# Weighing the values head by head, with four key blocks in the four column groups of TensorE

## The chip, the cores and the metric

The kernel runs on one core of a Trainium2 chip. The metric is the device time of one launch in microseconds. Three runs of the kernel before gave 10604.21, 10606.17 and 10610.16 us; their median is 10606.17.

## The reference, cut to what matters

One layer stack over x of shape [16, 512, 128]: attention with 16 heads of 8 channels, a mixture of 8 experts, a state-space block solved by 8 fixed-point turns, and the mixture once more, each behind a layer norm and added to x. The change touches the attention alone:

```python
scores = jnp.einsum('bhqd,bhkd->bhqk', q, k) * SCALE
weights = jax.nn.softmax(scores, axis=-1)
attn = jnp.einsum('bhqk,bhkd->bhqd', weights, v)
attn = attn.transpose(0, 2, 1, 3).reshape(B, T, D)
return attn @ out_w + out_b
```

## The kernel before, in words

The five engines each run their own program and meet at semaphores; nothing reorders them, so the order written in the loops is the order on each queue. A loop runs over the 16 batch elements. In each come the attention, the mixture, the state-space block (the longest part, with 8 turns), and the mixture again; the preparation of the next element's queries, keys and values (`start`, ten steps on VectorE) is laid into the last mixture.

The attention of one element has 512 tokens in four blocks of 128. A loop over h (steps 0 to 19) runs on TensorE, ScalarE and VectorE at once. In step h:

- TensorE scores head h (`score`, L492, four products into the banks 0 to 2 in turn), VectorE takes the row maxima (`rowmax`, L1292), and splits them into two bf16 parts (`split_max`).
- The maximum of head h-1 is turned (`turn_max`, L502) into two rows of bank 6 and copied beside the queries (`copy_max`), by ScalarE in the steps with even h (L937) and by VectorE in those with odd h (L1306), between the third and the fourth exp or row maximum.
- Head h-2 is scored again, keys down and queries across, with the maximum subtracted (`rescore`, L515, banks 3 and 4 in turn), and ScalarE takes the exp into `probsT` (`exp`, L945). A re-scoring waits for the exp two before it, since there are two banks.
- Queries and keys of head h+2 are turned into bank 5 (`turn_head`, L479) and ScalarE copies them to `heads` (`copy_head`, L932).

Weighing (`weigh`, L527) goes by four heads (HG = 4). When the probabilities of heads 4c to 4c+3 are there, the step has four visits, one for each block of 128 keys. A visit is four products of 512 columns, one for each head, with 32 columns of `vaug` as the stationary operand (8 value channels, a column of ones that gives the sum of the weights, and zeros). Head j of the four writes partitions 32j to 32j+31 of bank 7, so the four run side by side in the four column groups, and the four visits add up in the bank. Then ScalarE copies the bank to `oT` (`copy_out`, L950), TensorE turns its four blocks back into bank 7 (`turn_out`, L535), and VectorE divides by the sums (`normalise`, L1313 and L1316). After the last group the result is turned (L557), copied (L966) and projected (L561), and VectorE adds it to x (L1333).

The values are laid into `vaug` in step 9 of `start` (L1282 and L1284): the area was filled with zeros earlier, then the column of ones, then one copy of all heads.

Of the kernel before, what the change touches and what calls it, by code (L numbers as in the profile page):

```python
# [14 lines left out]
P = 128  # L15
# [8 lines left out]
TB = T // P  # L24
NH, HD = 16, 8
HG = 4
# [85 lines left out]
def hybrid_kernel(nc, t, out):  # L112

    with ExitStack() as ctx:
# [90 lines left out]
        probsT = piece(HG * TB * T).rearrange("p (j k t) -> p j k t", j=HG, k=TB)  # L205
# [58 lines left out]
        vchain = signal("vchain", 44, 8, 20)  # L264
# [12 lines left out]
        nchain = signal("nchain", 7)  # L277
# [20 lines left out]
        o_copied = signal("o_copied", NH // HG)  # L298
        o_turned = signal("o_turned", NH // HG)
        o_normed = signal("o_normed", NH // HG)  # L300
# [144 lines left out]
        def _(eng):  # L445
# [22 lines left out]
            def attention(at):  # L468
# [27 lines left out]
                def turn_max(h):  # L496

                    eng.wait_ge(max_parts.sem, max_parts.count(at, h + 1))
                    if h > 0:
                        eng.wait_ge(max_copied.sem, max_copied.count(at, h))  # L500
                    for tb in range(TB):
                        mm = eng.matmul(ps[BIAS:BIAS + 2, 6, tb * P:(tb + 1) * P],  # L502
                                        smax_b[:, h % 2, tb, :], ident_b[:],
                                        start=(tb == 0), stop=(tb == TB - 1))
                    mm.then_inc(max_turned.sem, max_turned.up(at))
# [391 lines left out]
        def _(eng):  # L897
# [26 lines left out]
            def attention(at):  # L924
# [10 lines left out]
                def copy_max(h):  # L935
                    eng.wait_ge(max_turned.sem, max_turned.count(at, h + 1))
                    eng.activation(heads[BIAS:BIAS + 2, h % QUAD, 0], ps[BIAS:BIAS + 2, 6, :],  # L937
                                   ACT.Copy).then_inc(max_copied.sem, max_copied.up(at))

                def exp(h, kb):  # L940
                    eng.wait_ge(rescored.sem, rescored.count(at, TB * h + kb + 1))
                    if h >= HG and h % HG == 0:

                        eng.wait_ge(weighed.sem, weighed.count(at, h - HG + kb + 1))
                    eng.activation(probsT[:, h % HG, kb, :], bank(3 + (TB * h + kb) % 2), ACT.Exp,  # L945
                                   scale=SCALE).then_inc(exped.sem, exped.up(at))

                def copy_out(c):
                    eng.wait_ge(weighed.sem, weighed.count(at, TB * (c + 1)))
# [4 lines left out]
                for h in range(NH + AHEAD + 2):  # L954
# [220 lines left out]
        def _(eng):  # L1175
# [31 lines left out]
            def start(at, step):  # L1207
# [71 lines left out]
                if step == 9:  # L1279

                    eng.wait_ge(v_zero.sem, v_zero.count(at, 1))
                    eng.memset(vaug[:, :, :, HD:HD + 1], 1.0).then_inc(nchain.sem, nchain.up(at))  # L1282
                    eng.wait_ge(nchain.sem, nchain.last(at))
                    eng.tensor_copy(  # L1284
                        vaug[:, :, :, 0:HD], qkv[:, :, 2 * DM:].rearrange("p b (h c) -> p b h c", c=HD)
                            ).then_inc(v_ready.sem, v_ready.up(at))

            def attention(at):
# [15 lines left out]
                def copy_max(h):  # L1304
                    eng.wait_ge(max_turned.sem, max_turned.count(at, h + 1))
                    eng.tensor_copy(heads[BIAS:BIAS + 2, h % QUAD, 0], ps[BIAS:BIAS + 2, 6, :]  # L1306
                                    ).then_inc(max_copied.sem, max_copied.up(at))

                def normalise(c):

                    eng.wait_ge(o_turned.sem, o_turned.count(at, c + 1))
                    o = blocks(7).rearrange("p b (j r) -> p b j r", r=32)
                    eng.reciprocal(rsum[:], o[:, :, :, HD]).then_inc(vchain.sem, vchain.up(at))  # L1313
                    eng.wait_ge(vchain.sem, vchain.last(at))
                    dst = attn[:, :, c * HG * HD:(c + 1) * HG * HD].rearrange("p b (j r) -> p b j r", r=HD)
                    eng.tensor_tensor(  # L1316
                        dst, o[:, :, :, 0:HD],
                        rsum[:].rearrange("p b (j o) -> p b j o", o=1).broadcast_to([P, TB, HG, HD]),
                        ALU.mult).then_inc(o_normed.sem, o_normed.up(at))

                for h in range(NH + AHEAD + 2):
# [8 lines left out]
                    if behind > HG and behind % HG == 1:  # L1330
                        normalise(behind // HG - 1)
                eng.wait_ge(projected.sem, projected.count(at, 1))
# [411 lines left out]
```

## Time and profile before

| | |
|---|---|
| median of three runs | 10606.17 us |
| the profiled execution itself | 10630.49 us |
| its span | 10628.6 us |
| mean granted TensorE clock | 0.958 |
| TensorE busy | 9367.1 us (88%) |
| VectorE busy | 9021.3 us (85%) |
| ScalarE busy | 7321.0 us (69%) |
| GpSimd busy | 6111.1 us (57%) |

The profile is of one execution. An engine's share is its busy time over the span; a product on TensorE is pipelined, so its record (0.39 us for a product of 512 bf16 columns) overlaps the next one's, and the pace is read from the starts. PEclk is the share of the full TensorE clock (2.4 GHz) that was granted; 0.50 is 1.2 GHz. An f32 product has two records, an f32 turned block one. The first element's attention lies between 43 and 125 us of the span and each later one about 661 us after the one before.

### The profile page before, as it was taken

The page shows a single profiled execution, that of the slowest core. Times are in us where ns is not written, and L with a number is a line of the kernel's source. Part 1 is how long each engine was busy: PE and PEld are TensorE (multiplying, and loading weights), DVE is VectorE, ACT ScalarE, POOL GpSimd, SP SyncE. Part 2 cuts the span into 40 slices and gives each one's busy share as a digit, 9 for nine tenths or more (in the row PEclk, how much of TensorE's full clock was granted, in tenths as well). Part 3 has the DMA queues.
Part 4 walks back from the last instruction along what each step waited for, and adds up shares of the span by engine and source line. Part 5 has one row for each costly group of instructions (what it writes and reads, how often), then busy time and mean ns, then how long its engine had stood idle before and what let it go on. Part 6 is the DMA issues. An engine that isn't in the chain of part 4 may idle for free.

```text
span 10628.6 us, 254158 instructions
## 1 busy us (share of the span) xinstructions
PE 9367.1 (88%) x86042; PEld 6259.7 (59%) x86042; DVE 9021.3 (85%) x16781; ACT 7321.0 (69%) x15068; POOL 6111.1 (57%) x4900
## 2 busy tenths in 40 slices
PE   7988889888898888988889888898888988889888
PEld 4656656566565665656656566565665656656566
DVE  6978979788797887978879798797987979879798
ACT  5867768677685776857767576675766857668576
POOL 1936728367293672926729277292762927639276
PEclk9999999999999999999999999999999999999999
DMA  0000000000000000000000000000000000000000
GB/s 21 0 3 1 1 3 0 3 1 1 3 0 3 1 2 3 0 3 1 2 3 0 3 1 1 3 0 3 1 1 3 0 3 1 2 3 0 3 1 3
DMA packets 648462, 23.40 MB, mean 2 GB/s; under 512 B 629185, under 2 KB 647250, under 8 KB 647506
## 3 DMA queue, kind: packets, MB, share of 16 engines
q1 hardware_dynamic: 647890, 16.11, 3.6%
q8 instruction: 318, 5.21, 0.2%
q14 instruction: 254, 2.08, 0.1%
HBM read 9.40 MB, written 4.19 MB: 1 GB/s over the span
## 4 chain that ended last, share of the span: by engine, by line
DVE 31%; PE 27%; issue 17%; POOL 15%; ACT 5%; DVEq 2%; DMA 1%; POOLq 1%; SPq 0%; ACTq 0%
DVE work L1563 15%; POOL work L1662 15%; DVE work L1553 6%; PE ps L579 4%; PE ps L584 4%; PE ps L594 3%; PE ps L527 2%; PE ps L515 2%; PE ps L788 1%; ACT da L945 1%; DMA hend<-work 1%; PE ps L492 1%; PE ps L654 1%; DVE stats L1185 1%; DVEq L1547 1%
## 5 line engine op out<-in xcount | busy, mean ns | idle before, releaser
L1662 POOL TENSOR_TENSOR work<-work,crep 128x512 f32<-128x512 f32 x4608 | 5767.5, 1275 | 4437.9 <-DVE work L1502 3820.5
L1061 ACT ACTIVATE scan_in<-du,bcn 128x256 f32<-128x256 f32 x8832 | 3685.7, 497 | 18.1 <-PE ps L788 13.6
L1563 DVE TENSOR_TENSOR_SCAN work<-da,hend,ps 128x256 f32<-128x256 f32 x4608 | 3037.4, 724 | 45.1 <-PE ps L788 22.3
L788 PE MATMUL ps<-w_ident,scan_in 128*128 128x128 f32 x18432 | 2722.0, 282 | 325.4 <-ACT scan_in L1061 111.3
L788 PEld LDWEIGHTS ps<-w_ident,scan_in 128*128 128x128 f32 x18432 | 2034.1, 143 | 1286.9 <-issue 724.3
L1553 DVE TENSOR_TENSOR_SCAN work<-da,ps 128x512 f32<-128x512 f32 x2048 | 2364.1, 1200 | 19.1 <-PE ps L788 2.4
L778 PE MATMUL ps<-work,w_sel 128*32 128x256 f32 x17792 | 1410.2, 393 | 157.0 <-POOL work L1662 146.2
L979 ACT ACTIVATE work<-ps,w_gate_b 128x512 f32<-128x512 f32 x512 | 351.8, 687 | 895.2 <-PE ps L579 894.7
L1292 DVE TENSOR_REDUCE smax<-ps 128x1 f32<-128x512 f32 x1024 | 661.1, 686 | 201.5 <-PE ps L492 197.5
L778 PEld LDWEIGHTS ps<-work,w_sel 128*32 128x32 f32 x17792 | 355.5, 108 | 619.3 <-POOL work L1662 370.3
L945 ACT ACTIVATE da<-ps 128x512 f32<-128x512 f32 x1024 | 572.9, 596 | 164.1 <-PE ps L515 157.4
L1393 DVE SCALAR_TENSOR_TENSOR work<-ps,w_up_b,work 128x512 f32<-128x512 f32 x512 | 377.8, 750 | 271.8 <-PE ps L584 225.4
L742 PE MATMUL ps<-w_ident,bcn 128*32 128x128 f32 x18432 | 579.8, 279 | 0.0
L579 PE MATMUL ps<-xnT,gate_w 128*128 128x512 f32 x1024 | 567.1, 637 | 0.0
L584 PE MATMUL ps<-xnT,up_w 128*128 128x512 f32 x1024 | 552.3, 622 | 0.0
L594 PEld LDWEIGHTS ps<-down_w,work 128*128 128x128 f32 x4096 | 489.8, 192 | 88.3 <-issue 68.9
L742 PEld LDWEIGHTS ps<-w_ident,bcn 128*32 128x32 f32 x18432 | 507.3, 112 | 47.0 <-issue 44.3
L1077 ACT ACTIVATE yscT<-ps 128x512 f32<-128x512 f32 x288 | 172.0, 597 | 502.9 <-PE ps L778 502.9
L594 PE MATMUL ps<-down_w,work 128*128 128x128 f32 x4096 | 501.0, 276 | 4.0 <-DVE work L1393 4.0
L1045 ACT ACTIVATE u_sb<-ps 128x512 f32<-128x512 f32 x256 | 153.0, 598 | 498.6 <-DVE du L1518 498.6
L723 PE MATMUL ps<-mix_y,yT 128*128 128x256 f32 x2048 | 485.5, 380 | 0.0
L515 PE MATMUL ps<-da 98*128 98x512 bf16 x1024 | 394.6, 389 | 102.5 <-ACT da L945 59.5
(201 smaller groups left out, 12259.1 us busy)
## 6 DMA issues: line engine op xcount, KB each, us to landing
hend<-work SPq DMA_DIRECT2D x2304, 1.0 KB, 1.8
x_in<-in_x SPq DMA_DIRECT2D x17, 256.0 KB, 2.8
out<-work SPq DMA_DIRECT2D x16, 256.0 KB
gate_w<-in_gate_w SPq DMA_DIRECT2D x1, 1024.0 KB, 5.4
up_w<-in_up_w SPq DMA_DIRECT2D x1, 1024.0 KB, 7.5
down_w<-in_down_w SPq DMA_DIRECT2D x1, 1024.0 KB, 9.4
w_w_zy<-in_w_zy SPq DMA_DIRECT2D x1, 256.0 KB
work<-in_w_mix SPq DMA_DIRECT2D x1, 256.0 KB
```

What stands on the lines that cost most here:

```text
L579: mm = eng.matmul(bank(u % 2), gate_w[:, e, f * P:(f + 1) * P], xnT[:], start=True, stop=True)
L584: mm = eng.matmul(bank(2 + u % 2), up_w[:, e, f * P:(f + 1) * P], xnT[:], start=True, stop=True)
L594: mm = eng.matmul(blocks(6 + e % 2)[:, tb, :], hid[:, e % 2, f, tb * P:(tb + 1) * P], down_w[:, e, f, :], start=(tb == 0 and f == 0), stop ...
L742: mm = eng.matmul(ps[GC * k:GC * (k + 1), bank + m // 2, c:c + P], bcn[:, hf, tb, 1, n:n + 1].broadcast_to([P, GC]), ident[:], start=(m % ...
L778: mm = eng.matmul(ps[GC * q:GC * (q + 1), 3, j % 2 * TH:(j % 2 + 1) * TH], w["sel"][:], prod[:, p % PROD, q % 2 * TH:(q % 2 + 1) * TH], st ...
L788: mm = eng.transpose(ps[:, bank, c:c + P], scan_in[:, m, tb, 2 * j + s].rearrange("p k c -> p (k c)"), ident[:])
L945: eng.activation(probsT[:, h % HG, kb, :], bank(3 + (TB * h + kb) % 2), ACT.Exp, scale=SCALE).then_inc(exped.sem, exped.up(at))
L1061: ins = eng.activation(scan_in[:, m, tb, :, k, :], du[:, hf, tb, :].rearrange("p (e c) -> p e c", c=GC), ACT.Copy, scale=bcn[:, hf, tb, 0, ...
L1292: eng.tensor_reduce(smax[:, h % 2, qb:qb + 1], bank(u % 3), AX, ALU.max).then_inc(maxed.sem, maxed.up(at))
L1553: eng.tensor_tensor_scan(hst[:, p % NHID, :], da[:, 0, 2 * p:2 * p + 2, :].rearrange("p s t -> p (s t)"), bank(RING[p % 4]), 0.0, ALU.mult ...
L1563: ins = eng.tensor_tensor_scan(hst[:, p % NHID, half], da[:, 1, 2 * p + s, :], ps[:, RING[p % 4], half], hend[:, 2 * p + s:2 * p + s + 1], ...
L1662: eng.tensor_tensor(prod[:, to, :].rearrange("p (s t) -> p s t", s=2), hst[:, p % NHID, :].rearrange("p (s t) -> p s t", s=2), crep[:, hf, ...
```

## The change

Weighing goes head by head. For head h the four products of a visit are its four blocks of keys, each in a column group of its own, so that the four groups hold partial sums. Three heads share bank 7 (HG = 3): head h has its 9 columns (8 channels and the sum) at 9 times (h mod 3) of the 32, zeros elsewhere, and the three add up in the bank. Sixteen heads make six groups (OUTS = 6), the last with one head. The probabilities stay in a ring of four heads (HR = 4). The turning multiplies by `sel`, four unit matrices of 32 stacked, which turns a block of tokens and adds the four partial sums at once, into 128 columns of bank 6; the turned maximum moves from bank 6 to bank 5. The copy of the values into `vaug` becomes three fills and three copies, one pair for each place.

In TensorE's loop `weigh(h-3)` stands after the second re-scoring of step h, from step 3 on; `weigh(15)` and the last two turnings stand behind the loop. Core of the diff:

```diff
-HG = 4
+HG = 3
+HR = 4
+OUTS = -(-NH // HG)
+HC = HD + 1
@@ TensorE
-                def weigh(c, kb):
-                    eng.wait_ge(exped.sem, exped.count(at, TB * (HG * c + HG - 1) + kb + 1))
-                    if c == 0 and kb == 0:
+                def weigh(h):
+                    eng.wait_ge(exped.sem, exped.count(at, TB * (h + 1)))
+                    if h == 0:
                         eng.wait_ge(v_ready.sem, v_ready.count(at, 1))
-                    if c > 0 and kb == 0:
-                        eng.wait_ge(o_normed.sem, o_normed.count(at, c))
-                    for j in range(HG):
-                        mm = eng.matmul(ps[32 * j:32 * j + 32, 7, :],
-                                        vaug[:, kb, HG * c + j, :], probsT[:, j, kb, :],
-                                        start=(kb == 0), stop=(kb == TB - 1))
+                    if h > 0 and h % HG == 0:
+                        eng.wait_ge(o_copied.sem, o_copied.count(at, h // HG))
+                    for kb in range(TB):
+                        mm = eng.matmul(ps[32 * kb:32 * kb + 32, 7, :],
+                                        vaug[:, kb, h, :], probsT[:, h % HR, kb, :],
+                                        start=(h % HG == 0), stop=(h % HG == HG - 1 or h == NH - 1))
                     mm.then_inc(weighed.sem, weighed.up(at))
 
                 def turn_out(c):
                     eng.wait_ge(o_copied.sem, o_copied.count(at, c + 1))
+                    if c > 0:
+                        eng.wait_ge(o_normed.sem, o_normed.count(at, c))
                     for tb in range(TB):
-                        mm = eng.transpose(blocks(7)[:, tb, :], oT[:, tb * P:(tb + 1) * P], ident[:])
+                        mm = eng.matmul(ps[:, 6, tb * GC:(tb + 1) * GC], oT[:, tb * P:(tb + 1) * P],
+                                        w["sel"][:], start=(tb == 0), stop=(tb == TB - 1))
...
-                for h in range(NH + AHEAD + 2):
+                for h in range(NH + AHEAD):
...
-                        if behind >= HG and behind % HG == 0:
-                            weigh(behind // HG - 1, b)
                         if 0 <= behind < NH:
                             rescore(behind, b)
+                        if b == 1 and behind >= 1:
+                            weigh(behind - 1)
                     if h + 2 < NH:
                         turn_head(h + 2)
-                    if behind > HG and behind % HG == 1:
+                    if behind >= HG + 1 and behind % HG == 1:
                         turn_out(behind // HG - 1)
-                eng.wait_ge(o_normed.sem, o_normed.count(at, NH // HG))
+                weigh(NH - 1)
+                turn_out(OUTS - 2)
+                turn_out(OUTS - 1)
+                eng.wait_ge(o_normed.sem, o_normed.count(at, OUTS))
@@ ScalarE
                 def copy_out(c):
-                    eng.wait_ge(weighed.sem, weighed.count(at, TB * (c + 1)))
+                    eng.wait_ge(weighed.sem, weighed.count(at, min(HG * (c + 1), NH)))
+                    if c > 0:
+                        eng.wait_ge(o_turned.sem, o_turned.count(at, c))
...
+                copy_out(OUTS - 1)
@@ VectorE, start step 9
-                    eng.memset(vaug[:, :, :, HD:HD + 1], 1.0).then_inc(nchain.sem, nchain.up(at))
-                    eng.wait_ge(nchain.sem, nchain.last(at))
-                    eng.tensor_copy(
-                        vaug[:, :, :, 0:HD], qkv[:, :, 2 * DM:].rearrange("p b (h c) -> p b h c", c=HD)
-                            ).then_inc(v_ready.sem, v_ready.up(at))
+                    v = qkv[:, :, 2 * DM:].rearrange("p b (h c) -> p b h c", c=HD)
+                    for j in range(HG):
+                        eng.memset(vaug[:, :, j:NH:HG, HC * j + HD:HC * (j + 1)], 1.0)
+                    for j in range(HG):
+                        ins = eng.tensor_copy(vaug[:, :, j:NH:HG, HC * j:HC * j + HD], v[:, :, j:NH:HG, :])
+                    ins.then_inc(v_ready.sem, v_ready.up(at))
```

`normalise(c)` on VectorE keeps its place behind the maxima of the step in which `turn_out(c)` stands, reads 27 columns a block (9 for the last group) from bank 6, and the last one stands behind the loop.

## Rows read from the trace of the kernel before

**Rows 1.** The page's chain that ended last: shares by engine, then by line.
```profile
DVE 31%; PE 27%; issue 17%; POOL 15%; ACT 5%; DVEq 2%; DMA 1%; POOLq 1%; SPq 0%; ACTq 0%
DVE work L1563 15%; POOL work L1662 15%; DVE work L1553 6%; PE ps L579 4%; PE ps L584 4%; PE ps L594 3%; PE ps L527 2%; PE ps L515 2%; PE ps L788 1%; ACT da L945 1%; DMA hend<-work 1%; PE ps L492 1%; PE ps L654 1%; DVE stats L1185 1%; DVEq L1547 1%
```
**Rows 2.** Windows of the first attention: length, busy of PE, PEld, DVE, ACT, POOL, clock.
```profile
60.00:67.00 7.00, 6.26 (x47) 3.02 (x44) 6.77 (x15) 6.95 (x12) 0.00 (x0) 1.00 0.00 1
67.00:74.00 7.00, 7.00 (x55) 1.93 (x55) 3.89 (x10) 4.12 (x8) 0.00 (x0) 1.00 0.00 0
111.00:115.00 4.00, 2.09 (x9) 0.67 (x9) 0.73 (x4) 3.59 (x8) 0.00 (x0) 1.00 0.00 0
115.50:118.50 3.00, 3.00 (x17) 0.80 (x20) 0.00 (x0) 0.60 (x1) 0.00 (x0) 0.50 0.00 0
```
**Rows 3.** Timeline of ScalarE, two quiet steps of the last element: start, length, line.
```profile
9979.83 2.16 ACT L945 ACTIVATE da<-ps 128x512 f32<-128x512 f32 x4
...
9982.78 1.67 ACT L945 ACTIVATE da<-ps 128x512 f32<-128x512 f32 x3
9984.47 0.59 ACT L937 ACTIVATE da<-ps 2x512 bf16<-2x512 f32 x1
...
9986.48 2.16 ACT L945 ACTIVATE da<-ps 128x512 f32<-128x512 f32 x4
```
**Rows 4.** Timeline, the end of the first attention, and one row of the last.
```profile
115.70 0.60 ACT L945 ACTIVATE da<-ps 128x512 f32<-128x512 f32 x1 [0.21 <-PE ps L515]
...
120.72 0.60 ACT L950 ACTIVATE work<-ps 128x512 f32<-128x512 f32 x1 [4.43 <-PE ps L527]
...
122.71 0.66 PE L557 MATMUL ps<-w_ident,work 128*128 128x128 f32 x4 [0.68 <-DVE work L1316]
...
10040.57 0.60 ACT L950 ACTIVATE work<-ps 128x512 f32<-128x512 f32 x1 [3.00 <-PE ps L527]
```
**Rows 5.** Groups by line: count, busy us, mean ns, idle before and its releaser.
```profile
L950 ACT ACTIVATE work<-ps 128x512 f32<-128x512 f32 x64 | 38.0, 593 | 68.0 <-PE ps L527 68.0
```
**Rows 6.** Timeline of TensorE in the first burst, and one row of the second.
```profile
68.32 0.38 PE L492 MATMUL ps<-da 96*128 96x512 bf16 x1
...
68.63 1.06 PE L527 MATMUL ps<-da,scan_in 128*32 128x512 f32 x8
...
69.63 0.39 PE L515 MATMUL ps<-da 98*128 98x512 bf16 x1
...
85.64 1.07 PE L527 MATMUL ps<-da,scan_in 128*32 128x512 f32 x8
```
**Rows 7.** Timeline of TensorE in a quiet step of the first element.
```profile
78.62 0.39 PE L502 MATMUL ps<-ident_b,smax_b 128*2 128x128 bf16 x4
78.94 0.39 PE L515 MATMUL ps<-da 98*128 98x512 bf16 x1
79.16 0.38 PE L492 MATMUL ps<-da 96*128 96x512 bf16 x1
...
79.60 0.61 PE L479 MATMUL ps<-ident_b,da 128*72 128x128 bf16 x8
80.05 0.38 PE L492 MATMUL ps<-da 96*128 96x512 bf16 x1
```
**Rows 8.** Timeline, step 2 of the first element: fourth exp, and the re-scoring it frees.
```profile
56.93 0.60 ACT L945 ACTIVATE da<-ps 128x512 f32<-128x512 f32 x1
...
57.59 0.39 PE L515 MATMUL ps<-da 98*128 98x512 bf16 x1
```
**Rows 9.** Timeline of TensorE in the state-space block: f32 products of 32 columns.
```profile
244.25 0.98 PE L714 MATMUL ps<-w_w_bc,yT 128*128 128x32 f32 x8
245.07 0.31 PE L788 MATMUL ps<-w_ident,scan_in 128*128 128x128 f32 x1
```
**Rows 10.** Timeline of VectorE before the second element's first row maxima.
```profile
702.81 0.43 DVE L1284 COPY scan_in<-scan_in 128x512 f32<-128x512 f32 x1
...
706.65 2.48 DVE L1292 TENSOR_REDUCE smax<-ps 128x1 f32<-128x512 f32 x4 [3.40 <-PE ps L492]
```

More of the change, by code:

```diff
@@ L262, in hybrid_kernel @@
         stored = signal("stored", behind=1, unit=16)
-        vchain = signal("vchain", 44, 8, 20)
+        vchain = signal("vchain", 46, 8, 20)
         class Norm:
@@ L297, in hybrid_kernel @@
         weighed = signal("weighed", NH)
-        o_copied = signal("o_copied", NH // HG)
-        o_turned = signal("o_turned", NH // HG)
-        o_normed = signal("o_normed", NH // HG)
+        o_copied = signal("o_copied", OUTS)
+        o_turned = signal("o_turned", OUTS)
+        o_normed = signal("o_normed", OUTS)
         a_turned = signal("a_turned", 1)
@@ L936, in copy_max @@
                     eng.wait_ge(max_turned.sem, max_turned.count(at, h + 1))
-                    eng.activation(heads[BIAS:BIAS + 2, h % QUAD, 0], ps[BIAS:BIAS + 2, 6, :],
+                    eng.activation(heads[BIAS:BIAS + 2, h % QUAD, 0], ps[BIAS:BIAS + 2, 5, :],
                                    ACT.Copy).then_inc(max_copied.sem, max_copied.up(at))
@@ L941, in exp @@
                     eng.wait_ge(rescored.sem, rescored.count(at, TB * h + kb + 1))
-                    if h >= HG and h % HG == 0:
-                        eng.wait_ge(weighed.sem, weighed.count(at, h - HG + kb + 1))
-                    eng.activation(probsT[:, h % HG, kb, :], bank(3 + (TB * h + kb) % 2), ACT.Exp,
+                    if h >= HR and kb == 0:
+                        eng.wait_ge(weighed.sem, weighed.count(at, h - HR + 1))
+                    eng.activation(probsT[:, h % HR, kb, :], bank(3 + (TB * h + kb) % 2), ACT.Exp,
                                    scale=SCALE).then_inc(exped.sem, exped.up(at))
                 def copy_out(c):
-                    eng.wait_ge(weighed.sem, weighed.count(at, TB * (c + 1)))
+                    eng.wait_ge(weighed.sem, weighed.count(at, min(HG * (c + 1), NH)))
+                    if c > 0:
+                        eng.wait_ge(o_turned.sem, o_turned.count(at, c))
                     eng.activation(oT, bank(7), ACT.Copy).then_inc(o_copied.sem, o_copied.up(at))
@@ L953, in attention @@
                 copy_head(1)
-                for h in range(NH + AHEAD + 2):
+                for h in range(NH + AHEAD):
                     behind = h - AHEAD
@@ L1305, in copy_max @@
                     eng.wait_ge(max_turned.sem, max_turned.count(at, h + 1))
-                    eng.tensor_copy(heads[BIAS:BIAS + 2, h % QUAD, 0], ps[BIAS:BIAS + 2, 6, :]
+                    eng.tensor_copy(heads[BIAS:BIAS + 2, h % QUAD, 0], ps[BIAS:BIAS + 2, 5, :]
                                     ).then_inc(max_copied.sem, max_copied.up(at))
@@ L1311, in normalise @@
                     eng.wait_ge(o_turned.sem, o_turned.count(at, c + 1))
-                    o = blocks(7).rearrange("p b (j r) -> p b j r", r=32)
-                    eng.reciprocal(rsum[:], o[:, :, :, HD]).then_inc(vchain.sem, vchain.up(at))
+                    n = min(HG, NH - HG * c)
+                    o = ps[:, 6, 0:TB * GC].rearrange("p (b r) -> p b r", r=GC)[:, :, 0:n * HC].rearrange(
+                        "p b (j r) -> p b j r", r=HC)
+                    eng.reciprocal(rsum[:, :, 0:n], o[:, :, :, HD]).then_inc(vchain.sem, vchain.up(at))
                     eng.wait_ge(vchain.sem, vchain.last(at))
-                    dst = attn[:, :, c * HG * HD:(c + 1) * HG * HD].rearrange("p b (j r) -> p b j r", r=HD)
+                    dst = attn[:, :, c * HG * HD:(c * HG + n) * HD].rearrange("p b (j r) -> p b j r", r=HD)
                     eng.tensor_tensor(
                         dst, o[:, :, :, 0:HD],
-                        rsum[:].rearrange("p b (j o) -> p b j o", o=1).broadcast_to([P, TB, HG, HD]),
+                        rsum[:, :, 0:n].rearrange("p b (j o) -> p b j o", o=1).broadcast_to([P, TB, n, HD]),
                         ALU.mult).then_inc(o_normed.sem, o_normed.up(at))
-                for h in range(NH + AHEAD + 2):
+                for h in range(NH + AHEAD + 1):
                     behind = h - AHEAD
@@ L1329, in attention @@
                         split_max(h)
-                    if behind > HG and behind % HG == 1:
+                    if behind >= HG + 1 and behind % HG == 1:
                         normalise(behind // HG - 1)
+                normalise(OUTS - 1)
                 eng.wait_ge(projected.sem, projected.count(at, 1))
```

6 lines of the change are left out of this document (3 added, 3 removed).

## The prediction

> **What bounds the kernel now.** I read the page's totals and its chain first. TensorE is the busiest (88% of the span), but the chain is shared: VectorE 31%, TensorE 27%, and of the attention lines only L527 (weighing) and L515 (re-scoring) reach 2% each [rows 1]. So the change touches one stage of each of the 16 batch elements, and that stage has to be read by itself. A batch element takes about 661 us; its attention runs from 43 to 125 us in the first.
>
> The stage's windows show two kinds of steps (a step is one turn of the head loop, h; it scores head h and re-scores head h-2). In the quiet ones, without weighing, ScalarE is busy 6.95 of 7 us and VectorE 6.77 [rows 2]: ScalarE sets the pace. A step in which it copies no maximum takes 2.95 us (first exp at 9979.83 to first exp at 9982.78), one with it 3.70 (to 9986.48), 3.33 on average [rows 3]. In the burst, where four heads are weighed in one step, TensorE is busy 7.00 of 7 us while VectorE has 3.89 and ScalarE 4.12 [rows 2]. Four steps with one burst take 17.0 us (a group of weighings at 68.63, the same group of the next four heads at 85.64), 4.25 a step [rows 6]. At the end nothing is left beside the last burst: the last exp begins at 115.70, ScalarE copies the result at 120.72, and the final turning begins at 122.71 [rows 4]. TensorE runs that burst at half clock, 0.50 granted from 115.5 to 118.5, that is 1.2 GHz, after four microseconds in which it was busy 2.09 of 4 [rows 2]. The last element keeps 2.4 GHz there, and its copy waits 3.00 us instead of 4.43 [rows 4]. The copies' idle time is 68.0 us in all [rows 5]; at 3.00 and about 4.45 that makes 14 slow tails and 2 fast ones.
>
> **The change, part by part.** It doesn't lessen the weighing: 64 products of 512 columns before and after. It spreads them, one group of four side by side per step from step 3 on, adds two rounds of copying, turning and normalising (6 for 4), and makes the turning a real product.
>
> *Weighing on TensorE.* In the burst a group starts 0.31 us after the score ahead of it (68.32 to 68.63) and the next product 1.00 us later (69.63), where two plain products stand 0.22 apart [rows 6, 7]. A group therefore costs 0.31 + 1.00 - 0.22 = 1.09 us. Its columns alone are 0.89 of it: its records last 1.06, and a plain product's record of 0.39 outlasts the next start by 0.17; 0.20 is the change from plain products to groups and back. I take 1.09 in the new place too, between a re-scoring and a score. Bounds: 0.89, and 1.3 if the 0.20 came twice.
>
> The Trainium skill, TensorEngine Tiling (Array Packing), Key Properties, says that changing the tiling mode drains TensorE, which speaks against sixteen separate visits. By that rule, and the trace agrees with its 0.20 us a visit, the sixteen weighings keep their 1.09 each; without a drain the sum would be 3.2 us an element less.
>
> *A step of TensorE.* I call R1 the start of a step's second re-scoring and R2 of its third. From R1: 0.31 to the weighing, 1.00 to the score, 0.31 to the turned maximum (as to the weighing), 0.32 to R2 (78.62 to 78.94) [rows 6, 7]: 1.94. From R2 three products of 0.22, the head's turning 0.45 (79.60 to 80.05), three more of 0.22 to the next R1 [rows 7]: 1.77. A step is 3.71 if nothing waits. ScalarE (2.95 or 3.70 [rows 3], and at most the 0.59 of a copied result [rows 5] more) and VectorE (6.77 us in a little over two quiet steps [rows 2], and some 0.2 for each step's share of normalising) are under that, so TensorE becomes the bound. One wait is added on it: re-scoring product 1 needs the previous head's last exp. On even steps ScalarE has the copied maximum between exps 2 and 3: R2, exp 0.43 later (the product's record is 0.39), the maximum 0.61 later and the last exp 0.61 after that (each takes 0.59 to 0.60), then 0.66 to the product it frees (56.93 to 57.59) [rows 3, 8]: 0.43 + 0.61 + 0.61 + 0.66 = 2.31 in place of 1.77. An even step is 1.94 + 2.31, or 4.24, an odd one 3.71.
>
> *The new turning.* Before it is four turned blocks in one load each; now four products with an f32 block of 128 columns loaded twice each. The nearest row is L714, 128x128 f32 against 32 columns: eight records, the next product 0.82 us after their start [rows 9]. It stands at the end of steps 6, 9, 12 and 15. Even steps hide 0.53 of it in ScalarE's wait, so 0.29 + 0.82 + 0.29 = 1.40 for the first three. Bounds: 0.44 each (the four turned blocks of before, at the 0.45 that eight smaller ones of a head take) and 1.0. The copy of the result (0.59) on ScalarE is new for two of the six; the weighing behind it waits for it by 0.17 once in steps 3 to 13.
>
> *Adding up.* R1 of step 3 is at 57.59 [rows 8] and stays there. Five even and six odd steps: 5 x 4.24 + 6 x 3.71 = 43.5, with 1.40 and 0.17: R1 of step 14 at 102.6. Step 14 even: R1 of 15 at 106.9; the weighing there waits for the copy until 107.3; R2 108.95, turning, R1 of 16 at 110.7; weighing and maximum, R2 112.3; exp, maximum, exp: the third exp of ScalarE at 113.95; R1 of 17 at 114.6; weighing, R2 115.9; last exp 116.9 to 117.5. Now a chain that is all new: copy 0.6 (118.0), weigh head 15 1.0 (119.0), turn 1.0 (120.0), and the last round of copy, turning, reciprocal and product, which before takes 1.99 (120.72 to 122.71) and 0.3 more with the longer turning: the final turning at 122.3, against 122.71 [rows 4]. So at full clock the gain is 0.4 us an element, and all of it is the slow clock that before paid (about 1.45 in 14 of 16). Against the two fast elements it loses 1.2.
>
> *The clock.* From 113 to 118 the laid-out TensorE is busy some 2.4 of 5 us, no more than in the stretch before which it fell before [rows 2]. I take it that it falls again, about when head 15 is weighed: 1.0 to 1.6 us, 1.3. Then an element loses 0.9 in 14 cases and 1.2 in 2: 15 us.
>
> *The values' preparation.* One fill and one copy become three and three on VectorE: four instructions more, each under the 0.43 of today's whole copy, so at most 1.7 us. VectorE then idles 3.40 us before its first maximum, waiting for TensorE [rows 10]. Nothing. The maximum's move to bank 5 moves no work; I price it at nothing, since its product and its copy stay where they are; were its copy to wait for a head's copy (1.0 us) it would add at most that in each step, and nothing in the change asks for that.
>
> Sum against the profiled execution, 10628.6 of span and 10630.5 in all: +15, 10645. The runs shown have their median 24 us under it, at 10606.2; the same 15 us give 10621.
>
> **The rivals.** The measurement tells about 0.2%, 21 us, from no change: 1.3 us an element.
> A, the clock stays up: TensorE has work in every step to the end. For it: the last element kept it. Against: 14 didn't, with the same busy share. -0.4 x 14 + 1.2 x 2 = -3: 10603.
> B, the weighing hides better than in the burst: its loads come early beside plain products and it costs its columns alone, 0.89. For it: the loads of a group are short and there are plain products on both sides to hide them. Against: the 0.31 and 1.00 of the groups now, which also stand between plain products [rows 6]. 0.20 x 16 = 3.2 an element, 51 less than the forecast: 10570. Faster.
> C, slower: the slow stretch falls over the new end chain, from the weighing of head 14 to the last turning. Weighings +0.9 twice, turnings +0.8 twice (their columns and loads again): 3.4, less the 0.4: 3.0 x 16 = 48, 10654. It decides from two of these four on. For it: the chain's gaps (copies of 0.6 between short products) leave TensorE less than half busy; against: it came back after 3.3 us before.
> D, the four groups don't run side by side: 2.6 us a head more, 656 in all, 11260. Against: L527 does so in the same groups now.
>
> **How the numbers follow.** Forecast 0.37, A 0.15, B 0.24, C 0.22, D 0.02. Likeliest 10621, which is no change that can be told (+0.14%); with the bounds of the turning (0.4 x 6 an element at most, partly hidden, about 1.5 x 16 = 24 either way) it has its own range of 10600 to 10645. Over B and C the range is 10563 to 10656. Faster: B, and a little of A, 0.26. Slower: C, D and the upper part of the forecast's range, 0.31. The same: 0.43.
>
> **What would show it.** Steps 3 to 13 at 4.24 and 3.71 in turn: the head copies of ScalarE (L932) tell. Near 3.33 or 3.7 throughout: B, the wait for the exp was wrong. TensorE's idle waits for the exp should grow only on even steps. L714's 0.82 should return in the new turning. The final turning of the first element (122.7 now) is the yardstick: at 122.3 with granted clock 1.00 around the last weighing is A, 123.6 with 0.50 is the forecast, beyond 125 is C. Wrong altogether if the stage outside attention moves.

## The result and the profile after

The changed kernel takes 10659.53 us, the median of 5 runs (10658.40 to 10668.38), against 10606.17 before (10599.39 to 10610.16): a ratio of 1.0053, interval 1.0039 to 1.0068. It is slower by 53 us where no change was forecast, and 3.5 us beyond the range. The profiled execution took 10668.38 (span 10666.5, mean granted clock 0.952 for 0.958), 38 us over the profiled one of before.

The page after, busy time by engine and then the chain's shares. They hardly differ from [rows 1]: the page as a whole doesn't tell where 53 us went.

```profile
PE 9434.6 (88%) x86554; PEld 6343.1 (59%) x86554; DVE 9036.0 (85%) x16913; ACT 7330.6 (69%) x15100; POOL 6116.0 (57%) x4900
...
DVE 33%; PE 29%; issue 17%; POOL 13%; ACT 3%; DMA 2%; DVEq 2%; POOLq 1%; SPq 0%; ACTq 0%
```

So I measured each stage in all 16 elements, from VectorE's and ScalarE's instructions at its two ends, and took means (us):

```
stage of an element                              before   after
first head copy to add of the projection          79.29   81.50
  of it: first head copy to final turning         76.7    77.56
first half of the first mixture                   17.94   18.39
end of an element to the next one's first copy     0.82    1.29
scan iterations, all eight                       374.25  373.64
rest of the state-space block (inputs, tail)      65.69   65.63
at half clock: end of attention                    3.05    5.73
at half clock: start of the first mixture          7.19   11.34
```

Attention is 2.21 us an element longer, 35 in all; 0.9 of the 2.21 lies ahead of the final turning, the rest behind it.

The body of attention. Timeline of TensorE in the first element after (start, length, engine, line, operands); L518 re-scores, L540 is the new turning, L495 scores. The first four L518 rows are R1, the start of the second re-scoring, of four steps in turn.

```profile
62.48 0.38 PE L518 MATMUL ps<-da 98*128 98x512 bf16 x1
...
66.12 0.39 PE L518 MATMUL ps<-da 98*128 98x512 bf16 x1 [0.20 <-ACT da L946]
...
66.74 0.39 PE L518 MATMUL ps<-da 98*128 98x512 bf16 x1
...
70.47 0.38 PE L518 MATMUL ps<-da 98*128 98x512 bf16 x1
...
73.52 1.03 PE L540 MATMUL ps<-w_sel,work 128*128 128x32 f32 x8
74.39 0.38 PE L495 MATMUL ps<-da 96*128 96x512 bf16 x1
...
75.05 0.38 PE L518 MATMUL ps<-da 98*128 98x512 bf16 x1
```

From 62.48 to 66.74 is an even step, 4.26 us (the row at 66.12 is not an R1: it is the re-scoring that waited for ScalarE's copied maximum, L946); to 70.47 an odd one, 3.73; to 75.05 an even one with a turning, 4.58. The turning's visit costs 0.87 (73.52 to 74.39). Medians over the 16 elements of steps 3 to 13 are 3.72, 4.26, 3.72, 4.58, 3.71, 4.26, 4.75, 4.26, 3.72, 4.58, 3.71, in sum 45.27.

The end of attention. Timeline of the first element after; this execution reached its first head copy 0.84 us later than the one of before (46.57 against 45.73), so 0.84 is to be taken off before a row is laid beside [rows 4].

```profile
117.71 1.08 ACT L954 ACTIVATE da<-ps 128x512 f32<-128x512 f32 x2 [0.72 <-PE ps L518]
118.68 0.60 ACT L961 ACTIVATE work<-ps 128x512 f32<-128x512 f32 x1
...
119.34 1.06 PE L530 MATMUL ps<-da,scan_in 128*32 128x512 f32 x8 [1.45 <-ACT work L961]
...
120.33 1.08 PE L540 MATMUL ps<-w_sel,work 128*128 128x32 f32 x8
121.45 0.60 ACT L961 ACTIVATE work<-ps 128x512 f32<-128x512 f32 x1 [2.16 <-PE ps L540]
...
122.12 1.88 PE L540 MATMUL ps<-w_sel,work 128*128 128x32 f32 x8 [0.71 <-ACT work L961]
...
124.50 1.12 PE L566 MATMUL ps<-w_ident,work 128*128 128x128 f32 x4 [0.50 <-DVE work L1331]
...
126.30 2.07 PE L570 MATMUL ps<-w_out_w,work 128*128 128x128 f32 x8 [0.69 <-ACT work L978]
...
128.41 0.69 DVE L1349 TENSOR_TENSOR x_res<-ps,x_res 128x512 f32<-128x512 f32 x1 [3.97 <-PE ps L570]
```

The same stretch before, from the projection on:

```profile
124.05 1.16 PE L561 MATMUL ps<-w_out_w,work 128*128 128x128 f32 x8 [0.69 <-ACT work L966]
125.24 0.69 DVE L1333 TENSOR_TENSOR x_res<-ps,x_res 128x512 f32<-128x512 f32 x1 [2.59 <-PE ps L561]
```

Three pieces run at nearly twice the length that they have at full clock: the last turning 1.88 for 1.08, the final turning 1.12 for 0.66 [rows 4], the projection 2.07 for 1.16. Windows of the two kernels (length, busy of PE, PEld, DVE, ACT, POOL, then the granted clock), after first and then before, say why:

```profile
115.00:119.00 4.00, 2.31 (x12) 0.46 (x12) 0.00 (x0) 3.26 (x7) 0.00 (x0) 1.00 0.00 0
119.00:123.00 4.00, 2.96 (x21) 2.03 (x21) 0.49 (x2) 0.88 (x2) 0.00 (x0) 0.89 0.00 0
123.00:127.00 4.00, 2.81 (x12) 2.27 (x13) 0.38 (x2) 1.33 (x2) 0.00 (x0) 0.50 0.00 0
127.00:131.00 4.00, 1.37 (x7) 1.08 (x6) 2.11 (x11) 0.84 (x2) 0.00 (x0) 0.50 0.00 0
```

```profile
119.00:123.00 4.00, 2.59 (x23) 0.96 (x16) 0.55 (x2) 0.60 (x1) 0.00 (x0) 1.00 0.00 0
123.00:127.00 4.00, 1.52 (x12) 1.09 (x10) 1.68 (x8) 1.88 (x2) 0.00 (x0) 1.00 0.00 0
127.00:131.00 4.00, 2.07 (x8) 1.47 (x9) 1.55 (x9) 1.76 (x3) 0.00 (x0) 0.72 0.00 0
```

Before, the slow stretch began under the burst [rows 2] and was over by 119; the final turning, the projection and the first products of the mixture had 2.4 GHz (in 15 of the 16 elements; in the last a slow stretch begins under the projection). After, the burst is gone, the clock falls about 122.1 (0.89 granted from 119 to 123 is 0.9 us at half), and all that chain runs at 1.2 GHz. So it goes in all 16 elements after. Only the last turning is caught to different extents: 1.88 us in the first element, 1.59 in the mean, 1.06 at full clock (a_warm below). The groups by line carry it over all elements (count, then busy us, mean ns of one, and idle before with its releaser); after, then before:

```profile
L518 PE MATMUL ps<-da 98*128 98x512 bf16 x1024 | 385.5, 384 | 54.3 <-ACT da L946 37.4 <-DVE da L1319 10.3 <-ACT da L954 3.7
L530 PE MATMUL ps<-da,scan_in 128*32 128x512 f32 x2048 | 272.7, 605 | 26.2 <-ACT work L961 23.2
...
L570 PE MATMUL ps<-w_out_w,work 128*128 128x128 f32 x128 | 33.2, 441 | 11.0 <-ACT work L978 11.0
...
L566 PE MATMUL ps<-w_ident,work 128*128 128x128 f32 x64 | 17.9, 435 | 8.1 <-DVE work L1331 8.1
...
L1349 DVE TENSOR_TENSOR x_res<-ps,x_res 128x512 f32<-128x512 f32 x16 | 11.1, 691 | 63.5 <-PE ps L570 63.5
```

```profile
L561 PE MATMUL ps<-w_out_w,work 128*128 128x128 f32 x128 | 19.0, 292 | 11.0 <-ACT work L966 11.0
...
L1333 DVE TENSOR_TENSOR x_res<-ps,x_res 128x512 f32<-128x512 f32 x16 | 11.1, 692 | 41.9 <-PE ps L561 41.9
L557 PE MATMUL ps<-w_ident,work 128*128 128x128 f32 x64 | 10.5, 286 | 10.8 <-DVE work L1316 10.8
```

VectorE's wait from the last normalisation to the add (L1349, before L1333) is 63.5 us in all for 41.9, that is 3.97 an element for 2.62. The 21.6 us between them lie in the final turning and the projection, at 435 and 441 ns a product for 286 and 292. L518 waits 37.4 of its 54.3 us behind the copied maximum (L946), and L530 waits 23.2, 1.45 an element, for the copy of the result ahead of head 15 (L961).

### The profile page after: what moved, and what is told of

Its sections match the earlier page's. It is cut to its first block, busy times and chain, and to the rows that moved or that the text cites. A ratio compares the mean times of both kernels' runs of the same rounds, so it can differ in the third digit from the quotient of the medians.

```text
span 10666.5 us, 255586 instructions
## 1 busy us (share of the span) xinstructions
PE 9434.6 (88%) x86554; PEld 6343.1 (59%) x86554; DVE 9036.0 (85%) x16913; ACT 7330.6 (69%) x15100; POOL 6116.0 (57%) x4900
## 3 DMA queue, kind: packets, MB, share of 16 engines
q14 instruction: 270, 2.21, 0.1%
## 4 chain that ended last, share of the span: by engine, by line
DVE 33%; PE 29%; issue 17%; POOL 13%; ACT 3%; DMA 2%; DVEq 2%; POOLq 1%; SPq 0%; ACTq 0%
DVE work L1579 17%; POOL work L1678 12%; DVE work L1569 6%; PE ps L588 4%; PE ps L593 4%; PE ps L603 3%; PE ps L530 2%; PE ps L518 2%; DMA hend<-work 2%; PE ps L495 2%; DVE stats L1197 1%; PE ps L797 1%; PE ps L663 1%; DVEq L1563 1%; PE ps L540 1%
## 5 line engine op out<-in xcount | busy, mean ns | idle before, releaser
L518 PE MATMUL ps<-da 98*128 98x512 bf16 x1024 | 385.5, 384 | 54.3 <-ACT da L946 37.4
```

Source lines behind the costliest of these rows:

```text
L518: mm = eng.matmul(bank(3 + u % 2), k[:, kb * P:(kb + 1) * P], q, start=True, stop=True)
```

## The experiments

Eight kernels ran, in two sets; each set has its own runs of the kernel before (medians 10626.87 of 21 runs, and 10614.0 of 15), and ratios are against these. The expected times were set against 10606.17; the first set's runs of before are 20.7 us higher, so there ratios are to be compared. By them b_warm and a_early lie in theory 1's range, a_warm just under its lower edge (0.9988 for 0.9989 to 1.0015), and a_own below both of its ranges (0.9976, and neither goes under 1.0004). The filler products in three of the eight are bf16 products of 512 columns into PSUM bank 1, which nobody reads at that time; they stand in TensorE's program where it would wait, and change only how busy it is.

**a_warm**: the changed kernel with fillers from the last re-scorings to behind the projection.

```diff
+                def busy(n):
+                    for _ in range(n):
+                        eng.matmul(bank(1), ident_b[0:BIAS, :], heads[0:BIAS, 0, 1], start=True, stop=True)
...
+                        if behind == NH - 1 and b == 0:
+                            busy(3)
...
+                busy(5)
                 weigh(NH - 1)
                 turn_out(OUTS - 2)
+                busy(2)
                 turn_out(OUTS - 1)
+                busy(2)
...
                 mm.then_inc(a_turned.sem, a_turned.up(at))
+                busy(2)
...
                 mm.then_inc(projected.sem, projected.up(at))
+                busy(11)
```

> The changed kernel, with idle stretches of TensorE at the end of each attention filled: 25 bf16 products of 512 columns (0.22 us each) whose result nobody reads, 3 ahead of the re-scoring of head 15, 5 ahead of the weighing of head 15, 2 ahead of the last turning, 2 ahead of the final turning, 2 ahead of the projection, 11 behind it. They add nothing to the computation. Theory 1 (the loss is the slow clock): the clock stays at 1.00 from the last weighing to the projection, the last turning, the final turning and the projection give back 0.9 + 0.46 + 0.91 = 2.3 us an element, attention falls from 81.5 to about 79.2 us and the start of the mixture with it: 10595 to 10622. Theory 2 (the loss is the new end chain and the longer turning by themselves, the slow clock comes along without costing): within 10 us of the changed kernel, 10650 to 10670.

Measured: 10610.61, ratio 0.9988 (0.9979 to 0.9997). Against the changed kernel's 1.0053 the fillers gain 0.65%. The same end, timeline of TensorE and VectorE of this kernel:

```profile
121.06 1.06 PE L540 MATMUL ps<-w_sel,work 128*128 128x32 f32 x8 [0.28 <-ACT work L972]
...
122.62 0.66 PE L575 MATMUL ps<-w_ident,work 128*128 128x128 f32 x4
...
123.97 1.16 PE L580 MATMUL ps<-w_out_w,work 128*128 128x128 f32 x8 [0.25 <-ACT work L989]
...
125.17 0.69 DVE L1360 TENSOR_TENSOR x_res<-ps,x_res 128x512 f32<-128x512 f32 x1 [2.60 <-PE ps L580]
```

The three pieces are back at 1.06, 0.66 and 1.16, and VectorE's wait for the add is 2.60. Attention is 1.91 us shorter an element than in the changed kernel (79.59), with no half clock at its end, and the start of the mixture 1.85 shorter (16.54). It is the slow clock, and nothing in the new products themselves, that lengthens these three pieces. The fillers took nothing in return here: the changed kernel's second element, where the clock fell only as the last turning ended, has 80.96, and less the 0.46 and 0.91 of the final turning and the projection that is 79.59.

**b_warm**: the same fillers in the kernel before, for what the clock costs there.

```diff
+                        if behind == NH - 1 and b == 0:
+                            busy(4)
...
                         turn_out(behind // HG - 1)
+                busy(2)
...
                 mm.then_inc(a_turned.sem, a_turned.up(at))
+                busy(2)
...
                 mm.then_inc(projected.sem, projected.up(at))
+                busy(11)
```

> The kernel before, with the same kind of filling at the end of each attention: 4 products ahead of the re-scoring of head 15, 2 ahead of the final turning, 2 ahead of the projection, 11 behind it. They add nothing to the computation. Theory 1: the last burst of weighing, at half clock in 14 of 16 elements, gives back 1.45 us there, and the start of the mixture some more: 10560 to 10585. Theory 2: 10600 to 10612, as before.

Measured: 10590.01, ratio 0.9963 (0.9949 to 0.9977). Groups by line of this kernel, the copied result and the add:

```profile
L959 ACT ACTIVATE work<-ps 128x512 f32<-128x512 f32 x64 | 38.0, 593 | 48.1 <-PE ps L527 48.1
...
L1342 DVE TENSOR_TENSOR x_res<-ps,x_res 128x512 f32<-128x512 f32 x16 | 11.1, 691 | 41.5 <-PE ps L569 41.5
```

ScalarE waits 48.1 us for the last burst, 3.0 in every element as I had read it from the one row of the last [rows 4], and 19.9 less than before [rows 5]: the prediction's reading of the burst at half clock was right. The add's wait is as before (41.5 for 41.9). With fillers in both, the changed kernel is the slower one by 0.25% (0.9988 to 0.9963, known to about 0.15%). This pair doesn't cut the 0.53% into order and clock, though, since the fillers work unequally behind attention: the start of the mixture takes 16.54 us in a_warm (2.13 at half clock) and 17.53 in b_warm (4.91), the same work in both, and that is 16 us in all to the changed kernel's credit. The stages of attention cut it better. With the clock up, attention takes 79.59 after against 77.86 before (so does the one element before, the eleventh, that kept its clock): the new order itself is 1.73 us longer. The slow clock costs 1.91 after (81.50 for 79.59) and cost 1.43 before (79.29 for 77.86), 0.48 net, and 0.45 net in the start of the mixture. Of the 3.1 us that an element grew in attention, in the mixture's start and at its end, 2.2 (35 us in all) are the order's 1.73 and the 0.47 at the element's end, which the fillers don't touch, and 0.9 (15 us) are the clock's.

**a_early**: the turned maximum directly behind the weighing, one product earlier.

```diff
-MAX_AT = 3
+MAX_AT = 2
...
-                        if b == MAX_AT - 1 and 1 <= h <= NH:
-                            turn_max(h - 1)
...
                             weigh(behind - 1)
+                        if b == 1 and 1 <= h <= NH:
+                            turn_max(h - 1)
```

> The changed kernel, with the turned maximum moved on TensorE from behind the third score to right behind the weighing (both in column groups, so one change of the array's use less), and its copy on ScalarE and VectorE one place earlier, ahead of the third exp or row maximum. Theory 1 with the step as the prediction laid it out: the wait of the second re-scoring for the copied maximum (0.53 on even steps) goes and 0.24 us of every step, steps 3 to 13 fall from 4.24 and 3.71 to about 3.47, some 6 us an element: 10550 to 10575. Theory 3 (ScalarE, at 3.33 a step and a copied result, bounds as soon as TensorE doesn't, or the maximum's split now comes too late): steps of 3.7 to 3.9, 10600 to 10630. No gain at all would say that the wait was no wait.

Measured: 10579.4, ratio 0.9959 (0.9945 to 0.9972), 0.94% under the changed kernel. Timeline of TensorE, one step of this kernel, L505 the turned maximum:

```profile
76.09 0.38 PE L518 MATMUL ps<-da 98*128 98x512 bf16 x1
76.40 1.06 PE L530 MATMUL ps<-da,scan_in 128*32 128x512 f32 x8
77.31 0.39 PE L505 MATMUL ps<-ident_b,smax_b 128*2 128x128 bf16 x4
77.62 0.39 PE L495 MATMUL ps<-da 96*128 96x512 bf16 x1
77.85 0.38 PE L518 MATMUL ps<-da 98*128 98x512 bf16 x1
...
79.61 0.38 PE L518 MATMUL ps<-da 98*128 98x512 bf16 x1
```

A step is 3.52 (76.09 to 79.61; 3.47 was expected), even or odd; with a turning 4.38 to 4.44. Two things went. The wait for the exp on even steps: ScalarE now finds the turned maximum earlier and copies it while it waits for the third re-scoring, no longer between the last two exps that the next head's second re-scoring waits for; the group of L518 waits 19.7 us for 54.3. And 0.18 in every step: from R1 to R2 (76.09 to 77.85) is 1.76 for 1.94. The weighing and the turned maximum both use only a part of the array's columns (32 and 2 in their rows); joined, the way from R1 to R2 is 0.31 + 0.91 + 0.31 + 0.23, where apart it was 0.31 + 1.00 + 0.31 + 0.32. I read it so that the change between such products and plain ones is paid at the ends of the pair and no longer at those of each. The Trainium skill, TensorEngine Tiling (Array Packing), Key Properties, has it that a change of the tiling mode drains TensorE; the trace fits that, by about 0.18 us a step saved when two such visits are joined, though no run tells a drain from another cost of the change. Attention is 76.09, 5.4 under the changed kernel, although its end is still slow (6.98 us at half clock, and the add waits the same 63.5).

**a_own**: the last group of heads (head 15 alone) gets places of its own, so its weighing and turning wait for nobody.

```diff
-                    if h > 0 and h % HG == 0:
+                    if h > 0 and h % HG == 0 and h < NH - 1:
                         eng.wait_ge(o_copied.sem, o_copied.count(at, h // HG))
...
-                        mm = eng.matmul(ps[32 * kb:32 * kb + 32, 7, :],
+                        mm = eng.matmul(ps[32 * kb:32 * kb + 32, 2 if h == NH - 1 else 7, :],
...
-                        mm = eng.matmul(ps[:, 6, tb * GC:(tb + 1) * GC], oT[:, tb * P:(tb + 1) * P],
+                        mm = eng.matmul(ps[:, 0 if c == OUTS - 1 else 6, tb * GC:(tb + 1) * GC],
+                                        (oT2 if c == OUTS - 1 else oT)[:, tb * P:(tb + 1) * P],
```

> The changed kernel, with the last group (head 15 alone) in places of its own: bank 2 for its weighing, its own copy, bank 0 for its turning, its own sums. So the weighing of head 15 doesn't wait for the copy of the fifth group, nor the last copy for the fifth turning, nor the last turning for the fifth normalising. Theory 2: the end chain shortens by one copy (0.6) and one gap (0.3 to 0.7), 0.9 to 1.3 us an element: 10638 to 10645. Theory 1: the same 0.9, but with the slow clock still over turning and projection; if the shorter chain ends ahead of the fall, up to 2 us more: 10610 to 10645.

Measured: 10606.59, ratio 0.9976 (0.9967 to 0.9985), 0.77% under the changed kernel. Timeline of its end:

```profile
118.00 1.07 PE L532 MATMUL ps<-da,scan_in 128*32 128x512 f32 x8 [0.96 <-ACT da L957]
119.00 1.97 PE L542 MATMUL ps<-w_sel,work 128*128 128x32 f32 x16
...
121.47 0.65 PE L569 MATMUL ps<-w_ident,work 128*128 128x128 f32 x4 [0.50 <-DVE work L1335]
...
122.81 2.08 PE L573 MATMUL ps<-w_out_w,work 128*128 128x128 f32 x8 [0.69 <-ACT work L981]
...
124.92 0.69 DVE L1353 TENSOR_TENSOR x_res<-ps,x_res 128x512 f32<-128x512 f32 x1 [3.51 <-PE ps L573]
```

Both turnings follow the weighing without a gap (119.00, sixteen records in 1.97) and in this element all of it up to and with the final turning is at 2.4 GHz; the clock falls just ahead of the projection (2.08). From the last weighing to the final turning is 3.47 (118.00 to 121.47) for 5.16 (119.34 to 124.50): 0.8 of the 1.7 is the clock, which left the last turning alone (1.88 for 1.08 in the changed kernel), and 0.9 the copy that no longer stands between the turnings. The weighing itself also waits 0.5 less (0.96 for 1.45). Attention is 79.16 in the mean, 2.3 under the changed kernel, more than was expected of the shorter chain (0.9 to 1.3): the chain has 1.4 of it (0.5 and 0.9), and the clock, which fell later, the other 0.9. The 0.77% is also more than the 53 us between the medians (10659.53 and 10606.59, 0.50%): the runs of the kernel before are 20 us apart in the two comparisons, so this gain is between 0.5% and 0.8%.

The second set began with the changed kernel again.

**after_again**: no edit.

> The changed kernel unaltered, beside the variants, since the kernel before moves by 0.2% from chip to chip (10606 and 10627 in two sets). Both theories: 0.4 to 0.7% slower than before, attention 81.5 us, with the clock at half over the last turning, the final turning and the projection.

Measured: 10667.83, ratio 1.0051 (1.0037 to 1.0065): the slowdown stands in a second set of runs, with the same 63.5 us of wait for the add and 5.82 us at half clock at an element's end.

**a_early_own**: the edits of a_early and a_own together.

> The changed kernel with both edits that helped alone: the maximum turned right behind the weighing, and the last group in places of its own. If the two gains are of waits alone they add up: attention from 81.5 by 5.4 and 2.3 to 73.8, ratio to before 0.988 to 0.991. If part of the second gain (2.3 where the chain itself is 0.9 shorter) is where the slow clock falls, that part may be lost or kept: 73.8 to 75.2, ratio 0.990 to 0.994.

Measured: 10500.42, ratio 0.9897 (0.9881 to 0.9912). Attention is 72.84: 8.7 under the changed kernel, where the two alone have 5.4 and 2.3. The 1.0 beyond their sum is again the clock: with both, the slow stretch ahead of the add shrinks to 1.22 us an element, and 11 of the 16 have none of it: they take 72.4 to 72.5, the others 73.4 to 73.9. The ratio is as expected, attention 1.0 below the 73.8. Group by line, the add:

```profile
L1353 DVE TENSOR_TENSOR x_res<-ps,x_res 128x512 f32<-128x512 f32 x16 | 11.1, 692 | 47.6 <-PE ps L573 47.6
```

**a_early_own_warm**: the same with the fillers of a_warm.

> The same with the idle stretches of TensorE at the end of each attention filled by 25 products nobody reads, as in the filled variant. Theory 1 (slow clock): the clock stays at 1.00 through the projection, 0.9 to 2.3 us an element more than without the filling, and 1.5 in the start of the mixture: ratio to before 0.985 to 0.990. Theory 2: no gain over the unfilled one; where fillers are in the way of a shorter chain, 0.2 to 0.4 us an element lost.

Measured: 10458.1, ratio 0.9856 (0.9841 to 0.9871). This is the version that beats both, by 1.4% the kernel before and by 1.9% the changed one (0.9856 over 1.0051). The page's totals and, from the groups by line, the add:

```profile
PE 9356.5 (90%) x86954; PEld 6324.5 (61%) x86954; DVE 9009.0 (86%) x16913; ACT 7316.6 (70%) x15100; POOL 6116.6 (59%) x4900
```

```profile
L1364 DVE TENSOR_TENSOR x_res<-ps,x_res 128x512 f32<-128x512 f32 x16 | 11.1, 692 | 41.5 <-PE ps L583 41.5
```

TensorE executes 400 products more than in the changed kernel and is busy 78 us less (46 more than in a_early_own). But attention stays at 72.85, where theory 1 expected a gain: the clock is up in all 16 elements, but each is 0.4 longer than the 72.44 that is the median of those that kept it without fillers. Here the fillers stand in the way of the shorter chain, by what theory 2 had priced. The gain over a_early_own is in the start of the mixture, 16.25 for 18.14.

**b_early**: the kernel before, with the turned maximum earlier as in a_early.

```diff
-MAX_AT = 3
+MAX_AT = 2
...
                             rescore(behind, b)
+                        if b == 1 and 1 <= h <= NH:
+                            turn_max(h - 1)
```

> The kernel before, with its maximum turned one place earlier (behind the second re-scoring) and copied ahead of the third exp or row maximum. The quiet steps are bound by ScalarE, 6.95 of 7 us busy, and in the bursts TensorE is busy throughout: no gain, within 0.15% of before. If it gained as the changed kernel did (0.8 to 0.9% against it), the wait for the copied maximum would have been there before the change as well.

Measured: 10597.98, ratio 0.9988 (0.9979 to 0.9997): nearly nothing. Steps 3 to 13 take 45.76 us for 46.06 (sums of medians), where in the new order they fall from 45.27 to 41.36. The earlier maximum alone is worth 0.12% in the old order, where ScalarE sets the pace of the quiet steps, and 0.94% in the new one, where TensorE does and waits for it. So the gain of a_early belongs to the new order, and that order, given its maximum early, beats the old one given the same: 0.9959 against 0.9988.

## Why the prediction was wrong, by its steps

**Which stage, and what bounds it: right.** The loss is in attention and just behind it; TensorE becomes the bound of its steps.

**Weighing 1.09 a visit, steps of 3.71 and 4.24: right.** Measured 3.71 to 3.73 and 4.26; the sum of medians of steps 3 to 13 is 45.27, forecast 43.5 + 1.40 + 0.17 = 45.1. The step with the extra wait for the copy (step 9) is 4.75 for 3.71 + 0.82 + 0.17 = 4.70. The added wait is on the even steps alone, behind L946. Rival B, a cheaper weighing beside plain products, falls: its hallmark, steps near 3.33 to 3.7 throughout, isn't there. What B asked for, 0.2 less a visit, came only when a_early joined two visits. Rival D falls with the 1.06 us that the eight records of a group still last, rival A with the 0.50 from 123 on.

**The turning 0.82: right**, 0.87. **The end chain at full clock: 0.4 to 0.5 short.** The last exp ends at 118.79 - 0.84 = 117.95 for 117.5, and the last but one turning begins at 120.33 - 0.84 = 119.49 for 119.0. 0.33 of it is there from step 3 on: its R1, 3.72 ahead of the one at 62.48, stands at 58.76, and less 0.84 at 57.92 instead of the 57.59 that I had left unmoved (0.27 in each of the other 15 elements). It comes from a pause of VectorE inside the first head's split of its maximum; timelines, after and then before:

```profile
52.22 0.17 DVE L1314 TENSOR_TENSOR smax_b<-smax,smax_b 128x4 bf16<-128x4 f32 x1 [0.35 <-DVE smax_b L1312]
```

```profile
51.06 0.17 DVE L1301 TENSOR_TENSOR smax_b<-smax,smax_b 128x4 bf16<-128x4 f32 x1
```

The two halves of the split stand on the same engine, and the diff leaves both alone. The pause is there in the first and the eleventh head of every element of every kernel with the new order (0.28 to 0.35, before 0.03); the steps around the eleventh head aren't longer for it. Its cause stays open.

**The values' preparation and the maximum's new bank, nothing: right as far as seen.** VectorE idles 3.85 us behind the preparation for the 3.40 of [rows 10]; timeline after, the second element's first maxima:

```profile
713.89 2.48 DVE L1305 TENSOR_REDUCE smax<-ps 128x1 f32<-128x512 f32 x4 [3.85 <-PE ps L495]
```

The end of an element to the next first head copy did grow, by 0.47 us (7 us in all), but with the same preparation it is 0.84 in a_own. It is ScalarE that starts late: its table load, ahead of the first head copy, begins 0.10 us behind TensorE's first turned head in every element before and in a_own, and 0.55 in the mean after (0.58 in a_warm, with its clock up). It follows the program's text and not the clock; why stays open.

**The clock: this is the step that failed, in size.** The mechanism was as put: the clock falls at the end of the laid-out order too, and in all 16 elements, also in the two that I had left fast. But I let it fall at the weighing of head 15 and charged 1.3 us, up to the final turning, where my sum stopped. It falls later, about 122.1, and lasts longer. In the first element it takes 0.8 from the last turning (1.88 for 1.08; 0.5 in the mean of the elements), 0.46 from the final turning (1.12 for 0.66) and 0.91 from the projection (2.07 for 1.16), 2.2 in all and 1.9 in the mean, and 0.45 net from the mixture's start behind. Up to the final turning that is 0.8 for my 1.3, and since the chain ahead of it was 0.45 longer than laid out, the yardstick reads 124.50 - 0.84 = 123.66, just the forecast's 123.6: two errors that cancel, and no sign of what comes behind. Behind it I had assumed the old 2.53 us to the add (122.71 to 125.24). They are 3.91. That is 1.4 us an element, 22 us, and with the mixture's 7 and the open 7 it makes the forecast's +15 into some +51; the scan iterations and the tail of the state-space block give back 0.7 us an element in the profiled execution (38), the medians say 53. Rival C had the time nearly right (10654) with the wrong place, and that is luck: it had the slow stretch over two weighings and two turnings, where only the last turning was slow, and nothing behind.

**The order at full clock: a second term too small.** My own rows give 122.3 against 122.71 less 1.45, a loss of 1.05 with the clock up; a_warm and b_warm give 1.73. Of the 0.7 between them 0.27 is VectorE's pause, 0.2 the steps 3 to 13 (45.27 for 45.07), the rest the chain behind. With the 0.47 that stood at nothing these are 1.2 us an element, about as much as the clock's two together: 0.8 in attention (1.9 in every element for 1.3 in 14 of 16) and 0.45 behind it. Two slips of the sums change little: I put 1.2 for that 1.05 against the two fast elements, and D's 2.6 us a head make 666 and not 656.

The cause of the clock's failure can be read off the forecast's own rows: the old burst was slow, and its slow stretch ended before the final turning, so the clock of everything behind it was part of what the old order bought. I priced what the slow clock would cost in the new place, and not that the old place had kept it away from the next one. a_warm and b_warm show what each place costs: the same three pieces return to 1.06, 0.66 and 1.16 with the clock up, attention gives back 1.91 us an element in the new order and 1.43 in the old, and what is left, 1.73, is the new order's own.

## What to carry to other kernels

A slow stretch of the clock is a cost that moves: when an edit takes away the work under it, lay the chain out up to the next stretch of dense products, past the stage's end, and price every product there at both levels. Filler products that nobody reads, put where TensorE would wait, tell what the clock is worth (here 0.37% and 0.65%), and may stay in where they are not in the way: in the shortest chain they cost 0.4 us an element where the clock would have held. Read their effect stage by stage, since two filled kernels need not have the same clock everywhere. And when an edit makes another engine the bound, first look what that engine now waits for and which of its visits can be joined: moving one visit, the four small products that turn the maximum, by one place gained 0.94% in the new order and 0.12% in the old.

## What the hardware showed that I had not expected

The clock fell without any long pause of TensorE ahead of it: it was busy 2.31 of the 4 us from 115 to 119 and 2.96 of the next 4, its longest wait there was the 1.45 us of the row at 119.34, and the clock was then at 0.50 through two more windows. In a_early_own the same chain, shorter by its two edits, kept 2.4 GHz to the projection in 11 of 16 elements, so edits that only shorten the way to the end won more together (8.7 us an element) than apart (5.4 and 2.3). And a pair of visits to parts of the array's columns (four f32 groups, then a bf16 product of two columns) cost 0.91 + 0.31, about 0.2 less than the two apart, though they write different banks.
